# Causal attention stage: reciprocals of the softmax sums transposed on VectorE before they are stored

## The chip, the cores and the metric

The kernel runs on one core of a Trainium2 chip. The metric is the device time of one execution, in microseconds (us). Before the change it is 2143.79 us, the median of 3 runs (2137.61 to 2145.15).

## The reference, cut to what matters

The program computes four transformer layers on an activation of 2 x 1024 x 128 in float32. The change lies in the attention of layer 2, 16 heads of 64 features with a causal mask, whose keys and values come from one shared latent:

```python
latent_kv = x @ w_kv_down
kv = latent_kv @ w_kv_up
k, v = (kv[..., :HD], kv[..., HD:])
q = (x @ w_q).reshape(Bx, Tx, N_HEAD, HEAD_SIZE)
scale = HEAD_SIZE ** (-0.5)
att = jnp.einsum('bqhd,bkhd->bhqk', q, k) * scale
att = jnp.where(causal, att, -jnp.inf)
att = jax.nn.softmax(att, axis=-1)
y = jnp.einsum('bhqk,bkhd->bqhd', att, v)
return y.reshape(Bx, Tx, HD) @ w_out
```

The kernel leaves the exponentials undivided, multiplies them with the values, and divides the product by the row sums at the end.

## The kernel before, in words

`causal_stage` walks over 8 pairs of heads and, in each, over the 2 sequences of the batch: 16 batches of work, which the texts number m = 0 to 15. An even m is the first sequence (b = 0) of a pair of heads, an odd m the second (b = 1). A batch has 4 steps n, and each step takes a short and a long tile of 128 query rows, whose lengths add up to the same number of columns. For each tile TensorE makes the scores (`score_part`), VectorE takes the maxima and masks (`maximum`), ScalarE makes exponentials with their sums (`exponential`), TensorE transposes the result in blocks through PSUM (`turn`), ScalarE and VectorE copy one half each back to SBUF (`move`), and TensorE multiplies with the values (`product`). Beside this, in most steps, two pieces of the next pair's projections are made (`project`). The order on each engine is written out by hand, and semaphores tie the engines together: TensorE signals finished scores with `s_full` and finished transposes with `t_full`.

ScalarE leaves the row sums in `rs`, one per partition (a query row of a tile), for 8 tiles and 2 heads. They have to be multiplied into `y`, where the query rows lie along the free axis. So at the end of a batch:

- VectorE (`invert`, L1909) takes the 128 x 16 reciprocals into `rinv`, between the last `move` of the batch and the first `maximum` over the next long tile.
- SyncE (`spread`, L1694) writes them to a buffer in DRAM, [16, 128] with the query rows along a row. Source and destination run across each other, so each element is a run of its own: 2048 of 4 bytes. It waits for that to land (`r_out`), and then reads the buffer back in two DMAs, each spread over 64 partitions, into `rrow` (L1703).
- GpSimd (`on_pool`, L1949) multiplies the two halves of `y` by `rrow` once they are there.

On SyncE's queue, `load_weights` for a later pair of heads (L1691) stands behind every second `spread`, and behind the last one stand the first loads of the next stage.

After the stage, `out_stage` (L1329) multiplies `y` with the output weights, 16 matmuls to each of four chunks of 512 columns. Chunks 0 and 1 belong to the first sequence, chunks 2 and 3 to the second: chunk 2 waits until GpSimd is done with the last batch.

Of the kernel before, what the change touches and what calls it, by code (L numbers as in the profile page):

```python
# [22 lines left out]
B = 2  # L23
# [1578 lines left out]
def causal_stage(nc, R, ctx, W, dram, lat, y):  # L1602
# [8 lines left out]
    sb = lambda n, s, d=F32: ctx.enter_context(nc.sbuf_tensor(pre + n, s, d))  # L1611
    sem = lambda n: nc.alloc_semaphore(pre + n)
    w, late = W.qkv, R.xc[:].rearrange("p c t -> p (c t)")[:, 0:T]
    q, k = sb("q", [128, 2, B, T]), sb("k", [128, 2, B, T])
    v = sb("v", [128, 2, B, 8, C])
    p = [sb("p_short", [128, 2, CW]), sb("p_long", [128, 2, T])]
    pT = [sb("pT_short", [128, 2, 4, 128]), sb("pT_long", [128, 2, 8, 128])]
    nm = sb("nm", [128, 4])
    rs = sb("rs", [128, B, 8, 2])
    rinv = sb("rinv", [128, B, 8, 2])  # L1620
    rrow = sb("rrow", [128, T])
    r_dram = nc.dram_tensor(pre + "r_dram", [B, 16, 128], F32, kind="Internal").ap()
    r_out, r_in = sem("r_out"), sem("r_in")
    w_loaded = [sem("w_loaded0"), sem("w_loaded1")]
    s_full, max_done, exp_done = sem("s_full"), sem("max_done"), sem("exp_done")
    t_full, t_a, t_d = sem("t_full"), sem("t_a"), sem("t_d")
    pv_done, pv_out, inv_done, y_done = sem("pv_done"), sem("pv_out"), sem("inv_done"), sem("y_done")
# [5 lines left out]
    PER_BATCH = PER_STEP // B  # L1633
# [3 lines left out]
    def place(n):  # L1637
        return n // PER_STEP, n % PER_STEP // PER_BATCH, n % PER_BATCH

    def row_tile(n, long):  # L1640
        return 7 - place(n)[2] if long else place(n)[2]

    def ends_batch(n):
        return n % PER_BATCH == PER_BATCH - 1
# [6 lines left out]
    def short_turns(n):  # L1651
        return turns(n, (0, 1), 0)

    def long_turns(n, hh):
        return turns(n, (hh,), 1)


    def pieces(n):
        hp, j = n // PER_STEP, n % PER_STEP
        if hp + 1 == STEPS or j >= PIECES // 2:  # L1660
            return []
        return [(hp + 1, 2 * j + i) for i in range(2)]
# [11 lines left out]
    def bank_of(what):  # L1674
        return 4 + number[what] % 2
# [4 lines left out]
    def scores_of(n, long):  # L1680
        return 2 * (2 * n + long)
# [5 lines left out]
    def on_sp(sp):  # L1687
        def load_weights(hp):
            sp.wait_ge(t_full, number["project", hp - 2, PIECES - 1] + 1)
            for i, n in enumerate(("q", "k", "v")):  # L1690
                sp.dma_start(w[:, hp % 2, i, :], dram[f"L2_w{n}"][:, hp * C:(hp + 1) * C]).then_inc(w_loaded[hp % 2], 16)  # L1691


        def spread(m):  # L1694
            b = m % B
            sp.wait_ge(inv_done, m + 1)
            sp.dma_start(r_dram[b].rearrange("a q -> q a"), rinv[:, b].rearrange("p t h -> p (t h)"),
                         allow_slow_non_contiguous=True).then_inc(r_out, 16)
            sp.wait_ge(r_out, 16 * (m + 1))
            if m:  # L1700
                sp.wait_ge(y_done, 2 * m)
            for hh in range(2):
                sp.dma_start(rrow[PH * hh:PH * hh + PH, :].rearrange("p (t q) -> p t q", q=128),  # L1703
                             r_dram[b:b + 1, hh::2, :].broadcast_to([PH, 8, 128])).then_inc(r_in, 16)

        sp.dma_start(late[:, T - 128:T], dram["late"]).then_inc(W.late_loaded, 16)
        load_weights(2)
        for hp in range(STEPS):
            for b in range(B):
                spread(hp * B + b)  # L1710
            if hp + 3 < STEPS:
                load_weights(hp + 3)
# [109 lines left out]
    def projected(hp, m):  # L1822
        if m < 8:
            b, t = chunk(m % 4)
            return (q if m < 4 else k)[:, hp % 2, b, t], PH ** -0.5 if m < 4 else 1.0
        b, t = chunk(m - 8)
        s = t.start // 128
        return v[:, hp % 2, b, s:s + 4, :].rearrange("p s c -> p (s c)"), 1.0

    def turned(what, src):  # L1830
        _t, n, long, heads, half = what
        blocks = row_tile(n, long) + 1
        dst = pT[long][:, heads[0]:heads[-1] + 1, 0:blocks, HALVES[half]]
        return dst, src[:, 0:len(heads) * blocks * PH].rearrange("p (h s t) -> p h s t", h=len(heads), t=PH)
# [49 lines left out]
    def on_dve(dve):  # L1884
        def move(what):
            bank = bank_of(what)
            dve.wait_ge(t_full, number[what] + 1)
            if what[0] == "project":
                dst, scale = projected(*what[1:])
                dve.tensor_scalar(dst, R.ps[:, bank, :], scale, None, ALU.mult).then_inc(t_d, 1)  # L1890
            else:
                dve.tensor_copy(*turned(what, R.ps[:, bank, :])).then_inc(t_d, 1)  # L1892


        def maximum(n, long, hh):
            tb = row_tile(n, long)
            a = scores_of(n, long) + hh
            dve.wait_ge(s_full, a + 1)
            if a >= 4:
                dve.wait_ge(exp_done, a - 3)  # L1900
            cols = (tb + 1) * 128
            if long:
                src = R.ps[:, 2 * hh:2 * hh + 2, :].rearrange("p a c -> p (a c)")[:, 0:cols]
            else:
                src = R.ps[:, 2 * hh + 1, 0:cols]
            dve.tensor_tensor_reduce(p[long][:, hh, 0:cols], src, late[:, T - cols:T], -1.0, LARGEST,  # L1906
                                     ALU.add, ALU.min, nm[:, a % 4:a % 4 + 1]).then_inc(max_done, 1)

        def invert(n):  # L1909
            b = place(n)[1]  # L1910
            dve.wait_ge(exp_done, scores_of(n, 1) + 2)
            if n >= 2 * PER_BATCH:
                dve.wait_ge(r_out, 16 * (n // PER_BATCH - 1))
            dve.reciprocal(rinv[:, b], rs[:, b]).then_inc(inv_done, 1)

        dve.wait_ge(W.late_loaded, 17)
        for m in range(1, PIECES, 2):
            move(("project", 0, m))
        maximum(0, 0, 0)
        maximum(0, 0, 1)  # L1920
        maximum(0, 1, 0)
        move(short_turns(0)[1])
        maximum(0, 1, 1)
        move(("project", *pieces(0)[1]))
        for n in range(PAIRS):
            if n + 1 < PAIRS:
                maximum(n + 1, 0, 0)
            move(long_turns(n, 0)[1])
            if n + 1 < PAIRS:
                maximum(n + 1, 0, 1)  # L1930
            move(long_turns(n, 1)[1])
            if ends_batch(n):
                invert(n)
            if n + 1 < PAIRS:
                maximum(n + 1, 1, 0)
                move(short_turns(n + 1)[1])
                maximum(n + 1, 1, 1)
                for x in pieces(n + 1)[1:2]:
                    move(("project", *x))

    def on_pool(pool):
        pool.memset(late[:, 0:T - 128], 0.0).then_inc(W.late_loaded, 1)
        for n in range(PER_BATCH - 1, PAIRS, PER_BATCH):
            hp, b, _j = place(n)
            pool.wait_ge(r_in, 32 * (n // PER_BATCH + 1))
            for th in range(2):
                pool.wait_ge(pv_out, 2 * (n // PER_BATCH) + th + 1)
                own = y[:, hp, b, th * CW:(th + 1) * CW]
                pool.tensor_tensor(own, own, rrow[:, th * CW:(th + 1) * CW], ALU.mult).then_inc(y_done, 1)  # L1949

    return Programs(sp=on_sp, pool=on_pool, pe=on_pe, act=on_act, dve=on_dve)


# [489 lines left out]
def build_program(nc, dram, out):  # L2443
# [112 lines left out]
    def second_half():  # L2556
# [19 lines left out]
        with ExitStack() as ctx:  # L2576
            y = tile(ctx, "y2", [128, HEADS // 2, B, T])
            stages += [causal_stage(nc, R, ctx, W2, dram, lat, y)]
            stages += [out_stage(nc, R, ctx, W2, 2, 0, "o2", lambda i, c: y[:, i, c // 2, chunk(c)[1]], HEADS // 2, W2.wo,
                                 lambda c: (W2.y_done, 4 * (HEADS // 2) - 2 + 2 * (c // 2)), after_causal)]  # L2580
# [106 lines left out]
```

## Time and profile before

| what | before |
|---|---|
| time, median of 3 runs | 2143.79 us |
| time of the profiled execution | 2142.62 us |
| its span, first to last instruction | 2140.8 us |
| TensorE busy | 1976.6 us, 92% |
| VectorE busy | 1562.8 us, 73% |
| ScalarE busy | 1401.6 us, 65% |
| GpSimd busy | 208.7 us, 10% |
| mean granted TensorE clock | 0.974 |

The profiled execution takes 1.8 us more than its span. The causal stage fills the span from 1114 us to 1648 us. In a row of a timeline the first two numbers are the start and the length in us, then follow the engine (PE is TensorE, PEld its weight load, DVE VectorE, ACT ScalarE, POOL GpSimd, SPq SyncE's queue), the line of the kernel, the operation and its tiles; in brackets stands the idle time of the engine just before and what ended it. Tiles of this stage begin with `ca`: `cap_long` and `cap_short` are the exponentials, `capT_*` their transposes, `carinv` and `carrow` the reciprocals before and after their way through `car_dram`.

### The profile page before, as it was taken

To read this page: it belongs to the slowest core of one execution; us is meant where nothing else is said; L and a number is where in the kernel's file an instruction comes from. 1 tells how busy PE (TensorE), PEld (TensorE's weight loads), DVE (VectorE), ACT (ScalarE), POOL (GpSimd) and SP (SyncE) were. 2 spreads that over 40 slices of the span, in tenths; PEclk is the share of its full clock that TensorE was granted. 3 is DMA by queue.
4 is the path that set the end of the run, shared out by engine and by line. 5 is a ranking of instruction groups with operands and counts; after the bars stand their busy time and mean duration, and the time that the engine had idled before them with its cause. 6 is when DMAs were issued, how large, how long until landed. Compare 5 with 4: busy or idle time off the path is not lost. (4 is left out here: it accounts for less than half of the span.)

```text
span 2140.8 us, 43376 instructions
## 1 busy us (share of the span) xinstructions
PE 1976.6 (92%) x17202; PEld 867.0 (41%) x17202; DVE 1562.8 (73%) x2221; ACT 1401.6 (65%) x2777; POOL 208.7 (10%) x388
## 2 busy tenths in 40 slices
PE   7999999999999899999989988889888889999998
PEld 4222222222223422222235666666665344444453
DVE  7999999999994699999566655556565455555553
ACT  4999999999996479989856666666665322222253
POOL 3011111101112411111000000000000200000000
PEclk7999999999999889999999999999999999999999
DMA  3010100101000110110100011111111145455510
GB/s 98 2 27 16 30 23 21 25 22 29 18 15 20 30 31 14 36 31 20 29 2 15 15 25 19 18 26 15 21 17 17 26 116 120 116 119 125 124 48 20
DMA packets 107017, 82.63 MB, mean 39 GB/s; under 512 B 54720, under 2 KB 89536, under 8 KB 102864
## 3 DMA queue, kind: packets, MB, share of 16 engines
q1 hardware_dynamic: 105872, 79.05, 16.0%
q8 instruction: 131, 2.15, 0.4%
q10 hardware_dynamic: 432, 0.56, 0.1%
q0 software_dynamic: 528, 0.43, 0.1%
q14 instruction: 54, 0.44, 0.1%
HBM read 62.98 MB, written 2.42 MB: 31 GB/s over the span
## 5 line engine op out<-in xcount | busy, mean ns | idle before, releaser
L1069 DVE TENSOR_REDUCE a0nm<-ps 128x2 f32<-128x1024 f32 x512 | 586.9, 1216 | 10.4 <-PE ps L936 8.2
L1047 ACT ACTIVATE a0p<-ps 128x512 f32<-128x512 f32 x1024 | 544.2, 599 | 60.2 <-PE ps L956 43.4
L970 PE MATMUL ps<-a0p,a0vst 128*32 128x256 f32 x4096 | 327.9, 392 | 27.4 <-ACT a0p L1047 14.0
L1069 DVE TENSOR_REDUCE a1nm<-ps 128x2 f32<-128x1024 f32 x256 | 294.7, 1217 | 6.9 <-PE ps L936 6.0
L1047 ACT ACTIVATE a1p<-ps 128x512 f32<-128x512 f32 x512 | 275.6, 596 | 34.2 <-PE ps L956 25.3
L956 PE MATMUL ps<-a0qm,a0k 32*128 32x512 bf16 x1024 | 277.0, 386 | 0.0
L2145 ACT ACTIVATE ex_s<-ps 128x512 f32<-128x512 f32 x128 | 76.5, 597 | 252.9 <-PE ps L2100 252.9
L936 PE MATMUL ps<-a0k,a0q 32*128 32x512 bf16 x1024 | 203.0, 394 | 18.0 <-DVE a0nm L1069 15.9
L2234 DVE TENSOR_TENSOR ex_su<-ex_s,ps 128x512 f32<-128x512 f32 x128 | 88.1, 688 | 115.2 <-PE ps L2104 114.7
L1750 PE MATMUL ps<-cak,caq 64*128 64x512 f32 (+3 forms) x768 | 172.2, 524 | 0.0
L970 PE MATMUL ps<-a1p,a1vst 128*32 128x256 f32 x2048 | 163.9, 392 | 6.4 <-ACT a1p L1047 5.5
L956 PEld LDWEIGHTS ps<-a0qm,a0k 32*128 32x128 bf16 x1024 | 79.3, 91 | 208.4 <-ACT a0p L1047 118.2
L936 PE MATMUL ps<-a1k,a1q 64*128 64x512 bf16 x512 | 149.0, 399 | 12.2 <-DMA a1q<-a1parts_sb 6.3
L956 PE MATMUL ps<-a1qm,a1k 64*128 64x512 bf16 x512 | 156.2, 385 | 0.0
L970 PEld LDWEIGHTS ps<-a0p,a0vst 128*32 128x32 f32 x4096 | 81.5, 108 | 155.5 <-ACT a0p L1047 70.4
L1852 ACT ACTIVATE cap_long<-cap_long,canm 128x1024 f32<-128x1024 f32 (+3 forms) x128 | 126.3, 986 | 22.3 <-DVE canm L1906 18.3
L1906 DVE CUSTOM_DVE_ANT_0 cap_long<-ps,xc_res 128x1024 f32<-128x1024 f32 (+3 forms) x128 | 130.1, 1017 | 5.2 <-PE ps L1750 4.6
L2100 PE MATMUL ps<-h_res,f2wg 128*128 128x512 f32 x256 | 130.7, 592 | 0.0
L2104 PE MATMUL ps<-h_res,f2wu 128*128 128x512 f32 x256 | 130.7, 592 | 0.0
L2088 PE MATMUL ps<-ex_hid,f2wd 128*128 128x512 f32 x256 | 130.5, 592 | 0.0
L1844 ACT ACTIVATE capT_long<-ps 128x512 f32<-128x512 f32 (+3 forms) x128 | 65.4, 511 | 97.9 <-PE ps L1777 84.6
L2245 DVE TENSOR_TENSOR ex_hid<-ex_su,ex_wb 128x512 f32<-128x512 f32 x128 | 88.6, 692 | 42.4 <-DMA ex_wb<-ex_w_dram 36.3
(324 smaller groups left out, 2511.6 us busy)
## 6 DMA issues: line engine op xcount, KB each, us to landing
ex_wb<-ex_w_dram SPq DMA_DIRECT2D x62, 512.0 KB, 6.2
carrow<-car_dram SPq DMA_DIRECT2D x32, 256.0 KB, 4.4
xc_res<-a0rec SPq DMA_DIRECT2D x15, 256.0 KB
a0q<-a0parts_sb SPq DMA_DIRECT2D x95, 32.0 KB, 2.0
a1q<-a1parts_sb SPq DMA_DIRECT2D x94, 32.0 KB
a0k<-a0parts_sb SPq DMA_DIRECT2D x90, 32.0 KB, 2.0
a1k<-a1parts_sb SPq DMA_DIRECT2D x84, 32.0 KB
f2wg<-in_ex_gate SPq DMA_DIRECT2D x32, 64.0 KB, 1.8
```

The source lines that it names most:

```text
L936: pe.matmul(R.ps[:, bank + d, :], q[rows, slot, rt, t0:t0 + 128], k[rows, slot, rt, hf * CW:(hf + 1) * CW], start=True, stop=True).then_in ...
L956: pe.matmul(R.ps[:, score_bank(n), :], k[rows, place(u)[3], rt, s * 128:(s + 1) * 128], qm[rows, u % 2, rt, :], start=True, stop=True).the ...
L970: last = pe.matmul(R.ps[32 * j:32 * j + 32, 6, cols], vst[:, g, s, j * HG // 4, :], p[:, s % 2, j, cols], start=(g == 0 and s == 0 and hal ...
L1047: act.activation(p[:, s % 2, e, :], R.ps[:, score_bank(n), :], ACT.Exp).then_inc(exp_done, 1)
L1069: dve.tensor_reduce(nm[:, u % 2, tb, 2 - 2 * z:4 - 2 * z, hf], R.ps[:, bank:bank + 2, :], X_AXIS, ALU.max, negate=True).then_inc(bank_free, 1)
L1750: last = pe.matmul(R.ps[:, 2 * hh + bank, 0:cols], q[rows, hp % 2, b, tb * 128:(tb + 1) * 128], k[rows, hp % 2, b, c * CW:c * CW + cols], ...
L1852: act.activation(row, row, ACT.Exp, bias=nm[:, a % 4:a % 4 + 1], scale=-1.0, accum_out=rs[:, b, tb, hh:hh + 1]).then_inc(exp_done, 1)
L1906: dve.tensor_tensor_reduce(p[long][:, hh, 0:cols], src, late[:, T - cols:T], -1.0, LARGEST, ALU.add, ALU.min, nm[:, a % 4:a % 4 + 1]).then ...
L2088: pe.matmul(R.ps[:, i % 4, :], wd[:, (i // 4) % 2, :], hid[:, i % 4, :], start=False, stop=True, skip_group_check=True).then_inc(d_done, 1)
L2100: pe.matmul(R.ps[:, G_BANK + 2 * (i % 2), :], wg[:, slot, :], h_chunk(R, c), start=True, stop=True)\
L2104: pe.matmul(R.ps[:, U_BANK + 2 * (i % 2), :], wu[:, slot, :], h_chunk(R, c), start=True, stop=True)\
L2245: dve.tensor_tensor(hid[:, i % 4, :], su[:, i % 2, :], wb[:, slot, c * CW:(c + 1) * CW], ALU.mult)\
```

## The change

The reciprocals are transposed on VectorE, in 32 x 32 blocks, into a new tile `rturn`. After that partitions 32i to 32i + 15 hold, for 16 pairs of tile and head, the 32 query rows 32i to 32i + 31 of a tile side by side. SyncE stores them with four DMAs, of 16 rows of 128 bytes each. The tile `rinv` is padded from 16 to 32 columns, and filled with ones once at the start, so that the transpose reads nothing undefined. A new semaphore `inverted` holds the transpose until the reciprocal has been written.

```diff
-    rinv = sb("rinv", [128, B, 8, 2])
+    rinv = sb("rinv", [128, B, 32])
+    rturn = sb("rturn", [128, B, 32])
...
-            sp.dma_start(r_dram[b].rearrange("a q -> q a"), rinv[:, b].rearrange("p t h -> p (t h)"),
-                         allow_slow_non_contiguous=True).then_inc(r_out, 16)
-            sp.wait_ge(r_out, 16 * (m + 1))
+            for i in range(4):
+                sp.dma_start(r_dram[b][:, 32 * i:32 * i + 32], rturn[32 * i:32 * i + 16, b]).then_inc(r_out, 16)
+            sp.wait_ge(r_out, 64 * (m + 1))
...
             if n >= 2 * PER_BATCH:
-                dve.wait_ge(r_out, 16 * (n // PER_BATCH - 1))
-            dve.reciprocal(rinv[:, b], rs[:, b]).then_inc(inv_done, 1)
-
+                dve.wait_ge(r_out, 64 * (n // PER_BATCH - 1))
+            dve.reciprocal(rinv[:, b, 0:16], rs[:, b].rearrange("p t h -> p (t h)")).then_inc(inverted, 1)
+            dve.wait_ge(inverted, n // PER_BATCH + 2)
+            dve.transpose(rturn[:, b], rinv[:, b]).then_inc(inv_done, 1)
+
+        dve.memset(rinv[:], 1.0).then_inc(inverted, 1)
```

On VectorE, at the end of batch m = 0, this stands in the program before (ISA is the maximum of L1906 and the read of its result):

```order
L1906 ISA cap_short,canm<-ps,xc_res 128x128
L1906 ISA canm 128x1
L1892 COPY capT_long<-ps 128x5x64
L1914 RECIPROCAL carinv<-cars 128x16
L1906 ISA cap_long,canm<-ps,xc_res 128x1024
L1906 ISA canm 128x1
```

And this in the program after, where line numbers are one higher:

```order
L1907 ISA cap_short,canm<-ps,xc_res 128x128
L1907 ISA canm 128x1
L1893 COPY capT_long<-ps 128x5x64
L1915 RECIPROCAL carinv<-cars 128x16
L1917 STREAM_TRANSPOSE carturn<-carinv 128x32
L1907 ISA cap_long,canm<-ps,xc_res 128x1024
L1907 ISA canm 128x1
```

The transpose stands between the reciprocal and the maximum over the next batch's first long tile.

On SyncE's queue, batches m = 0 and m = 1 stand so in the program before:

```order
L1697 DMA car_dram<-carinv 128x16x1
L1703 DMA carrow<-car_dram 64x8x128 x2
L1697 DMA car_dram<-carinv 128x16x1
L1703 DMA carrow<-car_dram 64x8x128 x2
L1691 DMA a2qkv<-in_L_wq 128x128
L1691 DMA a2qkv<-in_L_wk 128x128
```

And so in the program after:

```order
L1699 DMA car_dram<-carturn 16x32 x4
L1704 DMA carrow<-car_dram 64x8x128 x2
L1699 DMA car_dram<-carturn 16x32 x4
L1704 DMA carrow<-car_dram 64x8x128 x2
L1692 DMA a2qkv<-in_L_wq 128x128
L1692 DMA a2qkv<-in_L_wk 128x128
```

One store has become four, in the same place. Nothing else moves on this queue, and TensorE, ScalarE and GpSimd keep their order.

## Rows read from the trace of the kernel before

**Rows 1.** Page, part 4: shares of the chain that ended last, by engine.

```profile
PE 35%; ACT 6%; DVE 4%; issue 1%; DMA 1%; another core or an unknown queue 1%; POOL 0%; POOLq 0%; SPq 0%; DVEq 0%
```

**Rows 2.** Timeline of SyncE's queue: stores (L1697) and read-backs (L1703) of the reciprocals.

```profile
1159.00 0.39 SPq L1697 DMA_DIRECT2D car_dram<-carinv  x1
...
1189.83 0.38 SPq L1697 DMA_DIRECT2D car_dram<-carinv  x1
...
1222.72 0.38 SPq L1697 DMA_DIRECT2D car_dram<-carinv  x1
1233.41 1.26 SPq L1703 DMA_DIRECT2D carrow<-car_dram  x2
...
1591.24 0.37 SPq L1697 DMA_DIRECT2D car_dram<-carinv  x1
...
1619.26 0.37 SPq L1697 DMA_DIRECT2D car_dram<-carinv  x1
...
1646.56 0.37 SPq L1697 DMA_DIRECT2D car_dram<-carinv  x1
```

**Rows 3.** Stretches: busy us (instructions) of PE, PEld, DVE, ACT, POOL; clock, DMA, GB/s.

```profile
1158.73:1189.56 30.83, 27.15 (x404) 20.16 (x400) 19.21 (x49) 20.60 (x48) 2.51 (x2) 1.00 0.10 19
1222.45:1257.57 35.12, 29.75 (x404) 22.73 (x400) 19.11 (x48) 20.60 (x48) 2.50 (x2) 0.90 0.11 17
```

**Rows 4.** Timeline, 1226 to 1236 us: TensorE's transposes and who waits for them.

```profile
1229.64 0.71 PE L1777 MATMUL ps<-ident_res,cap_long 64*128 64x64 f32 x16
...
1233.39 0.60 ACT L1844 ACTIVATE capT_long<-ps 128x512 f32<-128x512 f32 x1 [2.88 <-DMA a0k<-a0parts_sb]
```

**Rows 5.** Chain in order of time, 1140 to 1240 us: start, us, what.

```profile
1230.52 2.89 another core or an unknown queue
...
1234.91 3.61 PE ps L1792 x32
```

**Rows 6.** Timeline, 1332 to 1335 us, in the store window of m = 5.

```profile
1332.39 0.47 PE L1777 MATMUL ps<-ident_res,cap_short 64*128 64x64 f32 x8
1332.79 1.97 PE L1792 MATMUL ps<-capT_long,cav 128*64 128x128 f32 x32
...
1334.17 0.38 ACT L1844 ACTIVATE capT_short<-ps 128x256 f32<-128x256 f32 x1 [1.97 <-PE ps L1777]
```

**Rows 7.** Timeline: TensorE at one place of the program, in batches 1 and 2.

```profile
1168.81 0.46 PE L1777 MATMUL ps<-ident_res,cap_short 64*128 64x64 f32 x8 [1.48 <-issue]
...
1198.29 0.46 PE L1777 MATMUL ps<-ident_res,cap_short 64*128 64x64 f32 x8
```

**Rows 8.** DMA: packets of the window 1222 to 1234 us, and two issues of the whole span.

```profile
DMA packets 2066, 0.03 MB, mean 3 GB/s; under 512 B 2064, under 2 KB 2064, under 8 KB 2064
...
ex_w_dram<-ex_wT SPq DMA_DIRECT2D x4, 128.0 KB, 2.4
```

**Rows 9.** Timeline of VectorE at the end of batch 0.

```profile
1158.73 0.24 DVE L1914 RECIPROCAL carinv<-cars 128x16 f32<-128x16 f32 x1
1159.20 1.22 DVE L1906 CUSTOM_DVE_ANT_0 cap_long<-ps,xc_res 128x1024 f32<-128x1024 f32 x1 [0.23 <-PE ps L1750]
1160.35 0.08 DVE L1906 DVE_READ_ACCUMULATOR2_ANT canm<- 128x1 f32 x1
```

**Rows 10.** Timeline, 1226 to 1236 us: a longer copy on VectorE.

```profile
1233.43 0.69 DVE L1892 COPY capT_long<-ps 128x512 f32<-128x512 f32 x1 [3.55 <-DMA a0k<-a0parts_sb]
```

**Rows 11.** Chain in order of time at the end of the stage.

```profile
1646.56 10.93 DMA car_dram<-carinv
...
1658.13 4.32 DMA carrow<-car_dram
...
1662.52 2.49 POOL y L1949 x2
```

**Rows 12.** Timeline, 1655 to 1690 us: TensorE in the output projection.

```profile
1654.74 7.03 PE L1329 MATMUL ps<-y,a2wo 128*128 128x512 f32 x16
...
1665.06 8.83 PE L1329 MATMUL ps<-y,a2wo 128*128 128x512 f32 x16 [3.29 <-POOL y L1949]
```

More of the change, by code:

```diff
@@ L1619, in causal_stage @@
     rs = sb("rs", [128, B, 8, 2])
-    rinv = sb("rinv", [128, B, 8, 2])
+    rinv = sb("rinv", [128, B, 32])
+    rturn = sb("rturn", [128, B, 32])
     rrow = sb("rrow", [128, T])
     r_dram = nc.dram_tensor(pre + "r_dram", [B, 16, 128], F32, kind="Internal").ap()
-    r_out, r_in = sem("r_out"), sem("r_in")
+    r_out, r_in, inverted = sem("r_out"), sem("r_in"), sem("inverted")
     w_loaded = [sem("w_loaded0"), sem("w_loaded1")]
```

## The prediction, made before the changed kernel ran

> **What bounds the kernel now.** I read the chain that ended last first, since only what stands on it can move the time. Over the span it has, beside the engines, 1% in "another core or an unknown queue" [rows 1]. The kernel has one core, so this is a wait that the profile can't explain. Followed in stretches of 50 us, the chain shows it at five places only, and all lie in the causal stage: at 1230.5, 1298.5, 1364.7, 1431.5 and 1500.3 us, 2.1 to 2.9 us long (the first of them in [rows 5]). That made me lay the queue of SyncE beside it. The store of batch 2 is issued at 1222.72 us and the read-back, which waits for it, at 1233.41: it takes 10.7 us for 8 KB [rows 2]. The unexplained wait, 1230.52 to 1233.41, is the tail of that window. The other four lie in the windows of m = 4, 6, 8 and 10 in the same way.
>
> What stalls? TensorE does its 16 transposes by 1230.35, and ScalarE, which has only to copy them, begins at 1233.39, after 2.88 us of idling. The tile that the bracket names as the releaser belongs to another layer, so the row tells no cause [rows 4]. In the window of m = 5 the transposes end at 1332.86 and TensorE goes on at full pace with the next 32 matmuls, yet ScalarE gets to copy only at 1334.17 [rows 6]. So it is not TensorE that stops: its signal of finished work arrives 1.3 us late while the store is out. In the even batches TensorE has nothing else in hand at that point, so there the same lateness idles all three engines.
>
> What it costs is seen by laying two stretches side by side that hold the same work, 404 matmuls each, from one reciprocal to the next: 30.83 and 35.12 us, and in the longer one the granted clock is 0.90 instead of 1.00 [rows 3]. So a stall costs twice: after it the clock falls to its lower level for a while, and 32 matmuls take 3.61 us [rows 5] instead of 1.97 [rows 6].
>
> The last place is the end of the stage. Store (10.93 us), read-back (4.32) and GpSimd (2.49) follow one another [rows 11], and TensorE, having done chunks 0 and 1 of the output projection, stands still for 3.29 us until GpSimd releases chunk 2. After this pause 16 matmuls take 8.83 us, and before it 7.03 [rows 12].
>
> **Term 1: the windows of 15 stores.** From the first store to the last pass 1646.56 - 1159.00 = 487.56 us [rows 2], for 15 batches. How long would they be undisturbed? There are three kinds.
> - Six even batches, m = 2 to 12: 1222.72 - 1189.83 = 32.89 [rows 2]. Three of the six have this length to 0.01, so I take it as undisturbed.
> - Seven odd ones, m = 1 to 13. The shortest but one is m = 1, at 30.83 [rows 2, 3]. It is disturbed too: the transposes of `cap_short` come 1168.81 - 1158.73 = 10.08 us after the reciprocal, and at the same place of the next batch 1198.29 - 1189.56 = 8.73 us after it, though both batches run the same instructions up to there [rows 7] (reciprocals start 0.27 us before the store's issue). The front is 1.35 us too long, with 1.48 us of idling in it. Undisturbed: 29.48.
> - The last two, which project nothing: 28.02 and 27.30 [rows 2]. I take 27.30 for both.
>
> Sum: 6 x 32.89 + 7 x 29.48 + 2 x 27.30 = 458.30. If the stores no longer disturb, the stage is 487.56 - 458.30 = 29.3 us shorter. As the lower end I take the lengths that were really seen, 30.83 for the odd batches and 28.02 + 27.30 for the last two: 468.47, a gain of 19.1.
>
> Does the new store disturb? The old window has 2064 packets under 512 B [rows 8]: 2048 elements and 16 completions. The new one has 64 rows and up to 64 completions. All other stores of the program have longer rows, and no unexplained wait is near them; the stores of the expert weights, 128 KB each, land in 2.4 us [rows 8]. I take it that nothing is left.
>
> Here the Trainium skill speaks against the change. Its page "DMA: Bandwidth & Descriptors", section "Specifications", says that transfers below 512 B make the DMA engine read, modify and write. Rows of 128 B are still on the wrong side of that line. No run here shows the rule itself; by count, 64 such writes are 1/32 of 2048, and 29.3 us would shrink to 0.9 us. If it isn't the count that matters, the third rival below follows.
>
> **Term 2: the end of the stage.** The old store is issued at 1646.56 [rows 2]. In its place comes the transpose, to about 1646.85, and four issues; one takes 0.38 us [rows 2], with the gaps between them I count 0.45, so to 1648.65. Landing, as with the stores of the expert weights, is 2.4 us [rows 8]: 1651.0. Two read-back issues (1.26 [rows 2]) and a landing of 4.32 lead to 1656.6, and GpSimd's 2.49 to 1659.1 [rows 11]. TensorE comes to chunk 2 only at 1654.74 + 7.03 = 1661.8 [rows 12]. 2.7 us of cover are left, so the whole pause goes: 3.29 + (8.83 - 7.03) = 5.1 us. At least the 3.29 goes. What is late next is TensorE's own work, the 64 matmuls of the projection.
>
> **Term 3: what VectorE gets.** A transpose of 128 x 32 at each batch's end, and the wait for its own reciprocal. Behind them stands the first `maximum` of the next long tile, on which ScalarE's exponential waits, and that is on the chain. VectorE idles 0.23 us there anyway, waiting for scores [rows 9]. One signal costs 0.03 us (reciprocal's end at 1158.97 to the store's issue at 1159.00 [rows 2, 9]). The trace has no transpose on VectorE. From below the nearest is the read of an accumulator, 0.08, from above a copy of 128 x 512, 0.69 [rows 9, 10]; I take 0.26, a little over the reciprocal of 128 x 16, which is the row nearest in size (0.24 [rows 9]). It adds 0.03 + 0.26 - 0.23 = 0.06 us, times 15: 0.9 us. The ends are 0 and 0.49 x 15 = 7.4.
>
> The skill's page "VectorE: DVE Perf Modes", section "The three transpose paths", has 311 ns for 128 x 128 in bf16. By that the term would be an estimated 1.7 us, and the forecast 0.8 us higher; no row here shows it.
>
> **At nothing:** the `memset` of 64 columns (at the start of the stage VectorE has nothing to do until the first projection is there); three more issues on SyncE's queue, some 1.3 us, against 8 us (10.7 less 2.4) that the queue waits less; the weights of later pairs, which leave earlier than now and are not waited for; the first loads of the next stage, the same. Should their cover be gone, they cost what the queue waits, under 1 us in all. GpSimd's products are waited for only at the stage's end.
>
> **Sum.** 2142.62 - 29.3 - 5.1 + 0.9 = 2109.1 us for the profiled execution. The median is 1.17 us above it: 2110. With the bounds of all terms, 19.1 + 3.3 - 7.4 = 15.0 up to 30 + 5.1 = 35 us: 2109 to 2129, and I think of 2104 to 2122 as this case's own range.
>
> **Rivals.**
> - *The late signals are only in profiled executions*, a side effect of recording 2064 packets and all matmuls. Then term 1 is no gain: 2143.8 - 5.1 + 0.9 = 2139.6. For it: TensorE's matmuls went on while its signal was late, and one matmul record in a window may be missing. Against it: the timed runs have a median of 2143.79, and the profiled one 2142.62. If recording cost 29 us, they would be near 2114. 10%.
> - *Part of it stays.* Four stores still write short rows, and delay the signals half as much: 2143.8 - 14.6 - 5.1 + 0.9 = 2125. 9%.
> - *Slower: VectorE's end of a batch becomes longer.* If the transpose takes the upper bound of 0.69, each batch gets 0.49 us between its last copy and the next maximum, 7.4 us in all. With the late signals staying, only term 2 stands against it: 2143.8 + 7.4 - 5.1 = 2146.1. It decides from 15 x (t - 0.20) > 5.1, a transpose of 0.54 us. 3%.
> - *The store doesn't do what it says* and is still cut into single elements, now in four DMAs. Then the three more issues lengthen the last window to about 12 us: 2143.8 + 1.3 + 0.9 = 2146. The program has 16 x 32 where it had 128 x 16 x 1, with both sides contiguous in the last dimension. 2%.
>
> **How the numbers follow.** The forecast has 76%, the rivals 10, 9, 3 and 2. A change under 0.5% of the time, 10.7 us, can't be told from none. Faster by more than that: forecast and second rival, 0.85, less a little for a forecast that falls short: 0.84. Same: first rival and the milder forms of the last two, 0.13. Slower: 0.03. To hold 8 in 10 the range takes in the forecast's own and most of the second rival's: 2104 to 2132.
>
> **What would show it.** In the profile after: all odd batches from m = 1 to 13 near 29.5 us between reciprocals, even ones at 32.9; no "unknown queue" on the chain; granted clock near 1.00 from 1230 to 1600 us; read-back issued about 4 us after the reciprocal instead of 11; packets under 512 B in a window down to about 130; no pause of TensorE before chunk 2, and its 16 matmuls near 7.0 us; the first maximum of a batch less than 0.1 us later. The prediction is wrong if the odd batches keep 33 to 35 us, or if they are short in the profile while the timed runs stay near 2140.

## The result, and the profile after

The changed kernel takes 2109.74 us, the median of 4 runs (2108.93 to 2111.62); the kernel before, in the same comparison, 2144.47 (2137.61 to 2146.93). The ratio is 0.9844, with a 95% interval of 0.9821 to 0.9868. The forecast was 2110. The profiled execution takes 2111.62 us, its span 2109.8 us; before they were 2142.62 and 2140.8.

The two stretches of [rows 3], again from one reciprocal to the next, in the profile after:

```profile
1161.61:1191.10 29.49, 27.16 (x404) 20.17 (x400) 19.38 (x50) 20.47 (x48) 2.52 (x2) 1.00 0.09 20
1223.99:1253.47 29.48, 27.15 (x404) 20.17 (x400) 19.38 (x50) 20.47 (x48) 2.53 (x2) 1.00 0.09 20
```

Both now have the length that was worked out for an undisturbed one, and the clock of the second is no longer 0.90 but 1.00. All seven odd batches take 29.46 to 29.49 us, the six even ones 32.88 to 32.92. The chain has no "unknown queue" any more, which answers to [rows 1]:

```profile
PE 37%; ACT 5%; DVE 4%; issue 1%; POOLq 0%; DVEq 0%
```

SyncE's queue, which answers to [rows 2], and the packets of the window 1224 to 1236 us, which answer to [rows 8]: 160 are under 512 B, where about 130 had been expected and 2064 stood before. The read-back is issued 3.85 us after the first store instead of 10.69:

```profile
1224.51 2.78 SPq L1699 DMA_DIRECT2D car_dram<-carturn  x4
1228.36 1.26 SPq L1704 DMA_DIRECT2D carrow<-car_dram  x2
```

```profile
DMA packets 1188, 0.58 MB, mean 49 GB/s; under 512 B 160, under 2 KB 1184, under 8 KB 1184
```

VectorE at the end of batch 0, answering to [rows 9]. The transpose fits into what was idle time; the maximum starts 0.47 us after the reciprocal, exactly as before:

```profile
1161.61 0.24 DVE L1915 RECIPROCAL carinv<-cars 128x16 f32<-128x16 f32 x1
...
1161.89 0.21 DVE L1917 STREAM_TRANSPOSE carturn<-carinv 128x32 f32<-128x32 f32 x1
1162.08 1.22 DVE L1907 CUSTOM_DVE_ANT_0 cap_long<-ps,xc_res 128x1024 f32<-128x1024 f32 x1
```

The end of the stage, answering to [rows 11, 12]: GpSimd is done at 1631.73, and TensorE runs 48 matmuls without a pause, 0.435 us each, until 1643.35:

```profile
1621.53 1.70 SPq L1699 DMA_DIRECT2D car_dram<-carturn  x4
...
1622.48 20.87 PE L1329 MATMUL ps<-y,a2wo 128*128 128x512 f32 x48
...
1624.24 1.26 SPq L1704 DMA_DIRECT2D carrow<-car_dram  x2
...
1629.24 2.49 POOL L1953 TENSOR_TENSOR y<-y,carrow 128x512 f32<-128x512 f32 x2 [24.48 <-DMA carrow<-car_dram]
```

One thing went against the forecast: the stage's first reciprocal comes 2.88 us later than before (1161.61 against 1158.73). 1.27 us of it is there before the stage begins. The rest arises in its first 16 matmuls, which take 5.49 us after and 3.88 before. From 1116 to 1118 us the granted clock is 0.50 after, TensorE's lower level, and 1.00 before. The first row is of the profile after, the second of the one before:

```profile
1115.58 5.49 PE L1734 MATMUL ps<-h_res,a2qkv 128*64 128x512 f32 x16 [2.33 <-PEq L2600]
```

```profile
1114.31 3.88 PE L1733 MATMUL ps<-h_res,a2qkv 128*64 128x512 f32 x16 [2.33 <-PEq L2596]
```

TensorE had paused for 2.33 us ahead of it in both. A later run (`e9_own_line` below) has everything that the changed kernel has up to this place, and takes 3.88 us again:

```profile
1115.12 3.88 PE L1739 MATMUL ps<-h_res,a2qkv 128*64 128x512 f32 x16 [2.33 <-PEq L2606]
```

In a second profile of the changed kernel itself they take 5.28. So the two values come and go from execution to execution, and no row ties the longer one to the change.

### The profile page after: what moved, and what is told of

It reads as the page before. It is cut to its first block and busy times, and to the rows that moved or that the text cites. A ratio compares the mean times of both kernels' runs of the same rounds, so it can differ in the third digit from the quotient of the medians.

```text
span 2109.8 us, 43441 instructions
## 1 busy us (share of the span) xinstructions
PE 1968.5 (93%) x17202; PEld 859.8 (41%) x17202; DVE 1565.9 (74%) x2238; ACT 1400.8 (66%) x2777; POOL 208.5 (10%) x388
## 5 line engine op out<-in xcount | busy, mean ns | idle before, releaser
L936 PE MATMUL ps<-a1k,a1q 64*128 64x512 bf16 x512 | 150.0, 402 | 11.2 <-DMA a1q<-a1parts_sb 6.3
```

Source lines behind the costliest of these rows:

```text
L936: pe.matmul(R.ps[:, bank + d, :], q[rows, slot, rt, t0:t0 + 128], k[rows, slot, rt, hf * CW:(hf + 1) * CW], start=True, stop=True).then_in ...
```

## The experiments

They form three groups, each on a chip of its own, and each with runs of the kernel before beside it: 2129.08, 2128.48 and 2134.14 us, where the first comparison had 2144.47. So the kernel before differs by 5.7 us between these three chips, and by up to 16 us from the first comparison, whose chip has no number on record. The changed kernel itself was run again in the second group only (2109.92); where a run of another group is compared with it, the text says so.

**Is the gain tied to the chip?** The changed kernel, run once more (second group).

> The changed kernel unchanged, as the reference for the other runs of this call. On the chip of the last runs the kernel before took 2129 us and not 2144, so what the stores cost differs from chip to chip. Theory: the changed kernel has no late signals anywhere, so it takes 2108 to 2112 us on any chip, and the gain is what the kernel before loses there: 19 us where that takes 2129, 34 where it takes 2144. Rival (chips differ in all of the program): the changed kernel moves along with the kernel before, and the ratio stays at 0.984.

It took 2109.92 us (2108.8 to 2111.53, 6 runs), the kernel before 2128.48, ratio 0.9917 (0.9905 to 0.993). The theory holds: the changed kernel takes the same on both chips, and the kernel before loses more on one than on the other, 34.7 us in the first comparison and 18.6 in this one.

**Is it the number of rows, or the transpose?** `r_rows` is the same buffer seen as 128 rows of 64 bytes, one for each partition. This kernel leaves out the transposition, so `y` meets its sums in the wrong order; the work on all engines is otherwise the same.

```diff
-            for i in range(4):
-                sp.dma_start(r_dram[b][:, 32 * i:32 * i + 32], rturn[32 * i:32 * i + 16, b]).then_inc(r_out, 16)
+            sp.dma_start(r_rows[b], rinv[:, b, 0:16]).then_inc(r_out, 16)
...
-            dve.transpose(rturn[:, b], rinv[:, b]).then_inc(inv_done, 1)
```

> The reciprocals are stored without a transpose, as 128 rows of 64 bytes, one per partition; the row buffer then holds them in the wrong order, so y is scaled by the wrong sums. It has the few-and-longer-rows part of the change and nothing of the transpose on VectorE. Theory (the number of small writes to DRAM delays TensorE's signals): odd batches 29.5 us, no late signal over 0.3 us, time as with the change, 2110 us within 3. If the transpose on VectorE costs something, it is faster than the change by 15 times that, at most 2 us. Rival (rows under 512 bytes are bad whatever their number, and 64 bytes are worse than 128): several late signals come back, 2115 us or more.

2108.28 us (2107.28 to 2109.48), against 2129.08: ratio 0.9906 (0.9891 to 0.9921). Odd batches take 29.48 to 29.49 us. The whole gain is there without the transpose and with rows of 64 bytes, so a row need not have 128 bytes. The maximum starts 0.47 us after the reciprocal here too; the transpose costs nothing that can be seen.

**Do the element writes bring the loss back?** The old store is put beside the four new ones, to a buffer that nobody reads. VectorE waits for it only before the reciprocal of two batches later; the read-back stands behind it on the queue.

```diff
+            if m < 15:
+                sp.dma_start(r_aside[b].rearrange("a q -> q a"), rinv[:, b, 0:16],
+                             allow_slow_non_contiguous=True).then_inc(aside, 16)
```

> The changed kernel, and beside its four stores the old store of 2048 single elements, to a buffer in DRAM that nobody reads, in batches 0 to 14, issued just before the four. Nobody waits for it but the read-back behind it on the same queue. Theory (the element writes themselves delay TensorE's signals): odd batches 31 to 35 us again, unexplained waits on the chain in most even windows, 28 us more than the change: 2138 us, within 6. Rival (the gain came from the shorter wait of SyncE's queue and an earlier read-back, or from the new program's alignment): 2110 to 2113 us.

2119.61 us (2115.43 to 2122.65) against 2129.08; the odd batches take 29.9 to 32.7 us. The stretches that answer to [rows 3]:

```profile
1162.46:1192.41 29.95, 27.14 (x403) 20.16 (x400) 19.39 (x49) 20.48 (x48) 2.52 (x2) 1.00 0.14 20
1225.30:1258.01 32.71, 28.82 (x403) 21.84 (x400) 19.30 (x49) 20.70 (x48) 2.51 (x2) 0.95 0.10 19
```

The direction is the theory's, the size is not: about 10 us instead of 28. But the number 28 came from another chip. Here the kernel before has only some 15 us of it (the experiment with exchanged buffers). The seven odd batches of this run are 11.2 us longer than undisturbed, and 2129.08 - 2119.61 = 9.5 us is left for the end of the stage and what this run lost less. It was run again on the third chip (the expectation has the landing at 9.8 us; in the first of these two runs the read-back was issued 10.6 to 11.4 us after the element store):

> The changed kernel with the old store of 2048 single elements beside the four, once more, as the reference for this call: 2048 elements, 16 neighbouring ones of 4 bytes to each 64 bytes of DRAM, each of the 16 from another partition. By the run before: landing 9.8 us after the issue, late signals in even windows, 2117 to 2122 us where the kernel before takes 2129.

2127.28 us (2121.34 to 2135.46, 10 runs) against 2134.14, ratio 0.998 (0.996 to 0.9999). That is more than expected, and 17 us over the changed kernel on the second chip. All odd batches together are 15.4 us longer than undisturbed. The late signal is back at its old place: the transposes end at 1231.02, and ScalarE copies 3.4 us later.

```profile
1230.30 0.72 PE L1783 MATMUL ps<-ident_res,cap_long 64*128 64x64 f32 x16
...
1234.40 0.60 ACT L1850 ACTIVATE capT_long<-ps 128x512 f32<-128x512 f32 x1 [3.23 <-DMA a0q<-a0parts_sb]
```

Writes whose data nobody uses bring most of the loss of the windows back; how much depends on the chip and on the run. What they also bring back is a read-back that is issued over 10 us late, and with it GpSimd's products. The last experiment below separates the two.

**The end of the stage alone.** The old store in the last batch only.

```diff
+            if m < 15:
...
+            else:
+                sp.dma_start(r_dram[b].rearrange("a q -> q a"), rinv[:, b, 0:16],
+                             allow_slow_non_contiguous=True).then_inc(r_out, 16)
```

> The changed kernel with the old store of 2048 single elements in the last batch alone (m = 15). Theory: only the end of the stage goes back: TensorE waits 3.3 us before chunk 2 and runs slower for a while after, 5 us more than the change: 2115 us, ratio 1.0024. Rival (the pause at the end is absorbed by the next stage): less than 1.5 us more, 2110 to 2111.

2115.45 us (2111.86 to 2117.63, 6 runs). That is 5.5 us over the changed kernel on the second chip (2109.92), and 7.2 over the kernel with rows of 64 bytes on the same chip (2108.28). Its batches are all undisturbed. In its timeline stand the pause and the slower matmuls after it, as in [rows 12], each a little smaller:

```profile
1620.84 14.00 PE L1329 MATMUL ps<-y,a2wo 128*128 128x512 f32 x32
...
1637.56 8.60 PE L1329 MATMUL ps<-y,a2wo 128*128 128x512 f32 x16 [2.72 <-POOL y L1958]
```

**Why only in even windows?** The kernel before, with the two DRAM buffers exchanged.

```diff
-            sp.dma_start(r_dram[b].rearrange("a q -> q a"), rinv[:, b].rearrange("p t h -> p (t h)"),
+            sp.dma_start(r_dram[1 - b].rearrange("a q -> q a"), rinv[:, b].rearrange("p t h -> p (t h)"),
...
-                             r_dram[b:b + 1, hh::2, :].broadcast_to([PH, 8, 128])).then_inc(r_in, 16)
+                             r_dram[1 - b:2 - b, hh::2, :].broadcast_to([PH, 8, 128])).then_inc(r_in, 16)
```

> The kernel before, with the two buffers in DRAM exchanged: even batches use buffer 1, odd ones buffer 0. If what the windows of even batches have in common is the place in the program (TensorE has nothing in hand when its signal is late), the unexplained waits stay in even windows (m = 0, 2, 4, 6, 8, 10, 12) and the odd batches are the long ones, 31 to 35 us. If it is the address of the buffer, they move to odd windows, and batches 2, 4, 6 to 12 become longer than 32.9 us while the odd ones go to 29.5.

One run, 2127.46 us. Followed in stretches of 50 us, the chain has its unexplained waits where they were, in windows of even batches:

```profile
1230.16 2.20 another core or an unknown queue
...
1360.18 1.92 another core or an unknown queue
...
1426.30 1.34 another core or an unknown queue
...
1490.68 1.91 another core or an unknown queue
```

The odd batches take 29.5 to 33.5 us, the even ones 32.89 throughout. So in this run it is the place in the program and not which of the two buffers is written. The odd batches sum up to 14.7 us over undisturbed, where the first profile had 27.6: this is nearly all of the difference between the two profiles, 15.2 us of span.

**Number of descriptors, or writes to DRAM?** Three kernels have another transfer in the place of the element store of `r_aside`: 1024 elements to DRAM, 2048 to SBUF, 2048 read from DRAM.

```diff
+                sp.dma_start(r_aside[b, 0:8].rearrange("a q -> q a"), rinv[:, b, 0:8],
...
+                sp.dma_start(s_aside[:, b, :, 0], rinv[:, b, 0:16],
...
+                sp.dma_start(s_aside[:, b], dram["L2_wq"][0:16, 0:128].rearrange("a q -> q a"),
```

> The changed kernel with 2048 single elements written to a spare tile in SBUF, not to DRAM, beside the four stores, in batches 0 to 14. Theory (it is the writes to DRAM that back up): these land within 4 us of their issue, no late signal, the time of the changed kernel within 2 us. Rival (it is the number of descriptors, wherever they write): unexplained waits in even windows and 10 to 28 us more.

> The changed kernel with 2048 single elements read from DRAM into a spare tile in SBUF beside the four stores, in batches 0 to 14. Theory (writes to DRAM): no late signal, the time of the changed kernel within 2 us. Rival (number of descriptors, or any traffic of elements with DRAM): unexplained waits in even windows and 10 to 28 us more.

2110.58 us (2109.86 to 2111.65) and 2109.78 (2106.77 to 2110.99), where the changed kernel takes 2109.92. No batch is disturbed in either, so 2048 short transfers alone cost nothing. The first row is the landing of the writes to SBUF, the second that of the reads:

```profile
DMA to landing us min/median/max: 2.9/3.2/4.1
```

```profile
DMA to landing us min/median/max: 6.3/6.3/6.8
```

These two runs can't tell the kind of transfer from how long it is out. In the windows of m = 0 to 12 of all profiles (the last two batches run in another order, and vary without such stores too), the first signal that comes over 0.25 us late is one for which ScalarE or VectorE would copy 7.9 us after the reciprocal, some 7.5 us after the store's issue. By then both transfers have landed. A signal earlier in the window is on time even in the kernel before, with the element store out: these transposes end at 1228.78, 6.1 us after the store of m = 2, and are copied at once.

```profile
1228.07 0.71 PE L1777 MATMUL ps<-ident_res,cap_long 64*128 64x64 f32 x16 [0.94 <-ACT cav L1842]
```

```profile
1228.81 0.60 ACT L1844 ACTIVATE capT_long<-ps 128x512 f32<-128x512 f32 x1 [0.80 <-PE ps L1777]
```

> The changed kernel with 1024 single elements (8 of the 16 columns) written to a spare DRAM buffer beside the four stores, in batches 0 to 14. Theory (a backlog of element writes delays TensorE's signals): the backlog drains in half the time, 4 to 5 us after the issue, before TensorE reaches the place without other work, 7.5 us after; so little is lost: 0 to 3 us over the changed kernel. Rival (each element write costs TensorE the same): half of what 2048 cost, 5 to 14 us.

2117.2 us (2116.14 to 2122.69): 7.3 us over the changed kernel. Here my expectation failed. Half the elements neither land in half the time nor cost little. In SyncE's queue the read-back follows 10.3 us after the element store (9.6 to 11.1 over 15 windows):

```profile
1223.31 0.38 SPq L1701 DMA_DIRECT2D car_aside<-carinv  x1
1223.73 5.95 SPq L1704 DMA_DIRECT2D car_dram<-carturn  x4
1233.59 2.23 SPq L1709 DMA_DIRECT2D carrow<-car_dram  x2
```

**What about the writes, then?** A time that does not fall with the number led to another theory: in the old layout 16 neighbouring elements share 64 bytes of DRAM, and each comes from another partition. Three layouts of the same store on the third chip, beside the repeated one above. In the order of the lines below, the elements lie 8 bytes apart, each partition's in 128 bytes of its own; 64 bytes apart; or as in the old layout, but two columns only. Their results follow in another order:

```diff
+                sp.dma_start(r_aside[b, :, :, 0], rinv[:, b, 0:16],
...
+                sp.dma_start(r_aside[b, :, :, 0].rearrange("a q -> q a"), rinv[:, b, 0:16],
...
+                sp.dma_start(r_aside[b, 0:2].rearrange("a q -> q a"), rinv[:, b, 0:2],
```

> 2048 single elements to DRAM in the order of the reference of this call, but 64 bytes apart, so that no two share 64 bytes. Theory C: lands in 3 to 6 us, no late signals, 2110 to 2112 us. Theory N: about 10 us, late signals, 2117 to 2122 us.

2109.28 us (2109.05 to 2109.68), no batch disturbed, though 2048 elements of 4 bytes go to DRAM. Landing is quick, and so this store too is over before the place where signals come late:

```profile
DMA to landing us min/median/max: 4.1/4.4/5.0
```

> 256 single elements to DRAM (2 of the 16 columns) in the layout of the reference of this call: again 16 partitions write to each 64 bytes. Theory C: still lands 6 us or more after the issue, and still some late signals, 2112 to 2120 us. Theory N: lands within 4 us, none late, 2110 us within 2.

2114.12 us (2113.92 to 2115.18): 256 elements in the old layout cost 4.8 us more than 2048 that lie 64 bytes apart. The read-back is issued 9.45 us after the store (8.7 to 11.0 over 15 windows), and in the same window ScalarE and VectorE again copy late, after 16 transposes that end at 1232.44:

```profile
1225.06 0.38 SPq L1701 DMA_DIRECT2D car_aside<-carinv  x1
...
1234.51 1.26 SPq L1709 DMA_DIRECT2D carrow<-car_dram  x2
```

```profile
1231.73 0.71 PE L1783 MATMUL ps<-ident_res,cap_long 64*128 64x64 f32 x16
...
1233.46 0.60 ACT L1850 ACTIVATE capT_long<-ps 128x512 f32<-128x512 f32 x1 [0.85 <-PE ps L1783]
1234.12 0.69 DVE L1898 COPY capT_long<-ps 128x512 f32<-128x512 f32 x1 [2.15 <-DMA a0q<-a0parts_sb]
```

> 2048 single elements to DRAM as in the reference of this call, but each partition writes its 16 elements, 8 bytes apart, into 128 bytes of its own. Theory C (1024 elements took as long to land as 2048, so the time goes with how many partitions write into the same stretch of DRAM, not with the number): lands in 3 to 6 us, no late signals, 2110 to 2112 us. Theory N (number of element writes to DRAM, with a fixed part): lands about 10 us after the issue, late signals, 2117 to 2122 us.

2109.74 us (2109.07 to 2111.43). One odd batch of seven is 0.4 us too long, and that arises 16 us after the reciprocal, behind the read-back. In time the theory is right, in the landing wrong: the read-back follows 13.1 us after the element store in the window of m = 2, the longest of 15, and 10.0 to 11.9 us in the others; with the old layout on this chip it is 11.3 to 12.3.

```profile
1225.06 0.56 SPq L1701 DMA_DIRECT2D car_aside<-carinv  x1
1225.66 6.13 SPq L1704 DMA_DIRECT2D car_dram<-carturn  x4
1238.17 1.26 SPq L1709 DMA_DIRECT2D carrow<-car_dram  x2
```

At the same place as above, and at the same time to 0.01 us, nobody waits for TensorE:

```profile
1231.73 0.71 PE L1783 MATMUL ps<-ident_res,cap_long 64*128 64x64 f32 x16
...
1232.48 0.69 DVE L1898 COPY capT_long<-ps 128x512 f32<-128x512 f32 x1 [0.52 <-PE ps L1783]
1232.51 0.58 ACT L1850 ACTIVATE capT_long<-ps 128x512 f32<-128x512 f32 x1
```

So two things must be held apart. The landing is slow with elements 4 or 8 bytes apart, be they of one partition or of many, and quick with 64 bytes between them; no other spacing was tried. Late signals of TensorE came only with the 4-byte layout, in which neighbouring elements are of different partitions. This last run carries the argument, as the only one in which another kind of store is still out at the place in question, as far as the late read-back tells, and no signal is late. It also has the read-back as late as the old store has, so neither the slow landing nor the late read-back makes the loss.

It differs from the old layout in three things at once, though: the partitions, the spacing of 8 bytes, and the stretch that is written, 16 KB instead of 8. Which of them counts is not shown. What connects such writes with TensorE's signals no view shows either, and it stays open.

## Why the prediction was right, point by point

- **Term 1, the store windows: predicted 29.3 us, at least 19.1.** From the first reciprocal to the last the stage took 1646.29 - 1158.73 = 487.56 us, and takes 1621.01 - 1161.61 = 459.40 now: 28.2 less. The undisturbed lengths taken from other batches, 32.89 and 29.48, came out to 0.03 us. The 1.1 us missing are in the last two batches, 28.05 + 27.66 where I had taken 27.30 twice; the stretch from 1560 to 1600 us has a clock of 0.92 in the profile after. They vary: the second profile of the changed kernel has 26.60 + 27.65. The cause was right too: the element writes do it without anyone waiting for them. But its size is not the kernel's alone. On the first chip of the experiments the same term was about 15 us, and the whole gain on the second was 18.6. That the forecast of a gain came true rests on comparing on a chip that loses as much as the profiled one; the forecast of the time, 2110, does not depend on it.
- **What the writes do.** "That nothing is left" of the disturbance was right, but I had argued it by count, 64 writes against 2048, and the count is not the reason: 256 of the old kind still cost 4.8 us more than 2048 that lie 64 bytes apart. Here the prediction had luck: fewer element writes in the old layout would not have been enough. The new rows land in time, the read-back being issued 2.7 to 4.3 us after the first store in all 16 batches; that they are harmless because neighbouring words come from one partition is a reading, and not shown. The rule of the Trainium skill on transfers below 512 B (page "DMA: Bandwidth & Descriptors", section "Specifications"), which I had weighed against the change, costs nothing here that can be seen: rows of 64 and of 128 bytes, both below that line, leave every odd batch at 29.5 us. No run shows the rule itself.
- **Term 2, the end: predicted 5.1 us.** From the last reciprocal to the end of the span there were 494.5 us, and there are 488.8: 5.7 less. The experiment on this term alone has 5.5 to 7.2. Pause and slower clock after it both went: 3.29 + 1.80 = 5.1 us, and the other 0.6 of the 5.7 is not accounted for.
- **Term 3, VectorE: predicted 0.9 us.** It is 0. The transpose takes 0.21 us, less than the 0.26 that I took and less than the Trainium skill's 311 ns ("VectorE: DVE Perf Modes", "The three transpose paths"), which is for another size and type.
- **Not in the sum:** 2.9 us lost up to the first reciprocal. 2142.62 - 28.2 - 5.7 + 2.9 = 2111.6 is the profiled time. The sum had 2109.1 for it, 2.5 us less. Being 0.3 us from the median, 2109.74, is luck: the profiled execution had been 1.17 us below the median before, and is 1.9 above it after. And the case's own range, 2104 to 2122, is not the one that the bounds of its terms give, 2109 to 2129.
- **The rivals.** That late signals exist only in profiled executions is refuted by the timed runs. Half of it staying, the longer end of a batch on VectorE, and a store still cut into elements did not occur.

## What to carry to other kernels

A wait on the chain that the profile cannot name should be laid beside the DMA queues: if it falls again and again into the window of one transfer, the transfer is the suspect even though nothing waits for it. In all four comparisons of this case it paid not to transpose by storing single elements to DRAM with different partitions writing neighbouring words; transpose on an engine first, or give each partition a run of its own. And to know what an undisturbed batch costs, compare batches that run the same instructions: the best of them, put together piece by piece, gave the new length to 0.03 us.

## What the runs showed of the hardware that was not expected

- 2048 elements of 4 bytes to DRAM, 64 bytes apart, land in 4.4 us (4.1 to 5.0). Side by side, on the same chip, 2048 let the read-back go only after 11.3 to 12.3 us, and 256 after 8.7 to 11.0. 1024, on another chip, took 9.6 to 11.1.
- With element writes to neighbouring words from different partitions still out, TensorE's signals to ScalarE and VectorE came up to 3.4 us late, and only those from some 7.5 us after the store's issue on. After the idling the granted clock was 0.90 over a batch. Element writes 8 bytes apart, out as long, did not do it. Element writes to SBUF and element reads from DRAM cost nothing, but had landed before (3.2 and 6.3 us).
- The same kernel took 2144, 2129, 2128 and 2134 us in the four comparisons. Between the two profiles, 14.8 of the 15.2 us lie between the first reciprocal and the last; the second of them has its two DRAM buffers exchanged. Kernels in which no batch is disturbed and the last store is a new one took medians of 2108 to 2111 us in all four.
